# Window attention of the first layer: softmax scaling moved behind the value sums

## The reference

```python
xw = xp.reshape(Bx, nW, window, C)
qkv = (xw @ qkv_w + qkv_b).reshape(Bx, nW, window, 3, heads, hd)
q, k, v = (qkv[:, :, :, 0], qkv[:, :, :, 1], qkv[:, :, :, 2])
attn = jnp.einsum('bnqhd,bnkhd->bnhqk', q * scale, k)
attn = attn + bias[None, None]
...
attn = jax.nn.softmax(attn, axis=-1)
out = jnp.einsum('bnhqk,bnkhd->bnqhd', attn, v).reshape(Bx, nW, window, C)
out = out @ pw + pb
```

## Time and profile before

| | |
|---|---|
| median of 3 runs | 1364.43 us (1363.96 to 1365.02) |
| the profiled execution, timed from outside | 1360.38 us |
| its span, first to last instruction | 1358.6 us |
| mean granted TensorE clock | 0.839 of full |
| PE busy | 970.4 us, 71% |
| DVE busy | 899.0 us, 66% |
| ACT busy | 677.4 us, 50% |
| POOL busy | 593.5 us, 44% |
| transfers | 86481 packets, 142.11 MB |

### The profile page before, as it was taken

The page is one execution under the profiler, slowest core; times in us unless marked ns, Lnnn a source line. Parts: engine busy times, 40 slices in busy tenths (PEclk is TensorE's granted clock), DMA queues, the critical chain, the costliest instruction groups (busy, mean ns, idle before and its releaser), DMA issues.

```text
span 1358.6 us, 16130 instructions
## 1 busy us (share of the span) xinstructions
PE 970.4 (71%) x5318; PEld 521.5 (38%) x5318; DVE 899.0 (66%) x1366; ACT 677.4 (50%) x1009; POOL 593.5 (44%) x585
## 2 busy tenths in 40 slices
PE   5464466877777624377667778778999987677784
PEld 5221234544444312133222223226888852223231
DVE  6572766565666545968888865755666677876861
ACT  3221245454554332357667466664344346566674
POOL 6377545677784164453711456650000034706210
PEclk7776688788887865569788798978999998899999
DMA  7713445545565119224213352635655633544400
GB/s 244 260 43 110 136 102 154 154 131 157 145 161 144 64 34 115 35 41 67 43 23 48 53 95 45 113 85 124 212 192 193 205 74 67 88 62 63 72 21 13
DMA packets 86481, 142.11 MB, mean 105 GB/s; under 512 B 14973, under 2 KB 43774, under 8 KB 86398
## 3 DMA queue, kind: packets, MB, share of 16 engines
q1 hardware_dynamic: 77726, 123.50, 37.8%
q0 software_dynamic: 8192, 16.79, 5.0%
q10 hardware_dynamic: 480, 0.79, 0.5%
HBM read 58.17 MB, written 40.37 MB: 73 GB/s over the span
## 4 chain that ended last, share of the span: by engine, by line
PE 30%; DVE 11%; ACT 8%; DMA 5%; issue 4%; SPq 4%; POOL 3%; DVEq 0%; ACTq 0%; POOLq 0%
PE PS L915 7%; PE PS L874 5%; ACT P L982 5%; PE PS L934 5%; PE PS L892 4%; SPq L495 4%; DMA KS<-MAG 3%; PE PS L854 3%; DVE MX L1721 2%; PE PS L840 2%; DVE XNT L1462 2%; POOL A L1298 2%; PE PS L674 1%; PE PS L679 1%; ACT MAG L982 1%
## 5 line engine op out<-in xcount | busy, mean ns | idle before, releaser
L1721 DVE TENSOR_REDUCE MX<-PS 128x2 f32<-128x1024 f32 x256 | 306.5, 1222 | 123.4 <-PE PS L854 117.8
L982 ACT ACTIVATE P<-PS 128x1024 f32<-128x1024 f32 x256 | 262.4, 1025 | 168.4 <-PE PS L892 163.6
L854 PE MATMUL PS<-KS,QS 62*128 62x512 f32 x512 | 140.4, 546 | 69.7 <-DVE MX L1721 54.9
L1298 POOL DMA_INDIRECT A<-Y1D,POS x64 | 62.2, 972 | 273.4 <-DMA Y1D<-YE 186.7
L892 PE MATMUL PS<-QS,KS 64*128 64x512 f32 x512 | 125.9, 488 | 71.5 <-ACT P L982 68.9
L874 PE MATMUL PS<-P,V 128*32 128x512 f32 x1024 | 156.3, 686 | 0.1
L854 PEld LDWEIGHTS PS<-KS,QS 62*128 62x128 f32 x512 | 54.2, 209 | 211.3 <-DVE MX L1721 112.3
L915 PE MATMUL PS<-XRH,WH 128*128 128x512 f32 (+1 forms) x276 | 104.1, 419 | 0.0
L892 PEld LDWEIGHTS PS<-QS,KS 64*128 64x128 f32 x512 | 54.0, 206 | 122.7 <-ACT P L982 113.6
L773 PE MATMUL PS<-XST,WB 128*128 128x512 f32 x184 | 99.5, 683 | 0.0
L1317 POOL DMA_INDIRECT XS1D<-XN,POS x64 | 62.3, 973 | 63.2 <-DVE MX L1721 40.4
(11 more groups left out here) (220 smaller groups left out, 1854.8 us busy)
## 6 DMA issues: line engine op xcount, KB each, us to landing
WH<-W1SD SPq DMA_DIRECT2D x23, 704.0 KB, 4.8
WS<-WD SPq DMA_DIRECT2D x64, 200.0 KB, 4.2
QS<-EH SPq DMA_DIRECT2D x64, 128.0 KB, 4.3
KS<-EH SPq DMA_DIRECT2D x60, 128.0 KB, 5.8
WB<-in_wb SPq DMA_DIRECT2D x23, 322.0 KB, 2.9
XS<-XS0D SPq DMA_DIRECT2D x23, 256.0 KB, 4.2
Y0D<-YE SPq DMA_DIRECT2D x23, 256.0 KB, 4.3
XS<-XS1D SPq DMA_DIRECT2D x23, 256.0 KB, 3.8
```

The lines of the kernel that those rows point to most:

```text
L854: signal(pe.matmul(PS[:, s % 4, :], QS[rows, u % 3, hp, 128 * t:128 * t + 128], KS[rows, u % 3, hp, :], start=True, stop=True), "ms")
L982: act.activation(*a, **k).then_inc(sem[name], 1)
L1298: pool.indirect_dma_start(dst[:, k, t, :], None, src, bass.IndirectOffsetOnAxis(pos[:, k, g:g + 1], 0)).then_inc(sem[name], 16)
L1721: go("mx", dve.tensor_reduce(MX[:, u % 2, t].rearrange("p (o h) -> p o h", o=2)[:, :, hp], PS[:, s % 4 - 1:s % 4 + 1, :], AX.X, ALU.max))
```

## The change

The unscaled exponentials are spread. The sums and their reciprocals go to a new tile `REC` (two turns) instead of `WM`, and `even` is gone on both engines. A new function on SP, `spread_recips`, copies the reciprocals to the feature partitions in `RW`, again by seven and four transfers, now with rows of 20, 30 or 40 numbers. `window_out` multiplies the sums of the values by `RW` on VectorE, behind each of its two reductions. `spread` waits for the exponential where it waited for `even`. `window_max` of the next batch waits for the subtraction instead of `even`.

The table `MOVED` is changed as well. In the period of batch 4 the orders are now these. SP: store 14, passing 16, split 4, spread 4, spread_recips 4, store 15, passing 17, store 16, passing 18, store 17. GpSimd: large subtraction 4, products (4, 2), small subtraction 4, split 4, products (5, 0), norm step, products (5, 1), nine multiplications 4 (the two for the small windows each one place later). TensorE: head sum (5, 0) stands behind both halves of pass 17 instead of ahead of them; all else is as before. VectorE: the evacuation of head sum (5, 0) stands behind the clip of pass 17 instead of ahead of the tail's norm product. ScalarE: the weight split's copy stands one step earlier, ahead of the evacuation of sorted rows. Before batch 2, the split of weights 0 on GpSimd stands two scattering transfers earlier.

```diff
-LESS_AT, EXP_AT, SUM_AT, EVEN_AT, SPREAD_AT, OUT_AT = 11.5, 12, 13, 13.5, 14, 20
+LESS_AT, EXP_AT, SUM_AT, SPREAD_AT, RECIP_AT, OUT_AT = 11.5, 12, 13, 14, 15, 20
...
-            put(period * b + EVEN_AT, ("even", b, r))
...
+            REC = sb0("REC", [128, 2, 2, 40])
+            RW = sb0("RW", [128, 2, max(GRP)])
...
-        def even(eng, go, r, b):
-            eng.wait_ge(sem["wsum"], b + 1)
-            t = window_rows(r, b)
-            go("weven" + ("_v" if b < EARLY else ""),
-               eng.tensor_tensor(t, t, bc(WM[:, r], [128, 40, WIN[r]], 2), ALU.mult))
...
-                made(sp, "weven", b, 2)
+                sp.wait_ge(sem["wexp"], b + 1)
...
+            def spread_recips(b):
+                sp.wait_ge(sem["wsum"], b + 1)
+                for r in (1, 0):
+                    if b:
+                        sp.wait_ge(sem[f"wout{r}"], b)
+                    for s in range(4):
+                        rows = slice(32 * s, 32 * s + 32)
+                        if r:
+                            for p in range(2 if s < 3 else 1):
+                                at = WIN[1] * (4 * p + s)
+                                load(RW[:, 1, at:at + WIN[1]], bc(REC[rows, b % 2, 1, WIN[1] * p:WIN[1] * (p + 1)], [32, 4, WIN[1]], 1), "rec1")
+                        else:
+                            n, at = WIN[0] * (TURN0 + (s == 3)), WIN[0] * TURN0 * s
+                            load(RW[:, 0, at:at + n], bc(REC[rows, b % 2, 0, 0:n], [32, 4, n], 1), "rec0")
...
+                elif (what, *a[1:]) == ("window", RECIP_AT):
+                    spread_recips(a[0])
...
-                    made(dve, "weven", b - 1, 2)
+                    made(dve, "wsub", b - 1, 2)
...
-                    ins = dve.tensor_reduce(WM[:, r], window_rows(r, b), AX.X, ALU.add)
+                    ins = dve.tensor_reduce(REC[:, b % 2, r], window_rows(r, b), AX.X, ALU.add)
                 step(ins)
-                go("wsum", dve.reciprocal(WM[:], WM[:]))
+                go("wsum", dve.reciprocal(REC[:, b % 2], REC[:, b % 2]))
...
-                go(f"wout{r}", dve.tensor_reduce(WO[r][:], wide, AX.X, ALU.add))
+                step(dve.tensor_reduce(WO[r][:], wide, AX.X, ALU.add))
+                dve.wait_ge(sem[f"rec{r}"], 16 * (4, 7)[r] * (b + 1))
+                go(f"wout{r}", dve.tensor_tensor(WO[r][:], WO[r][:], RW[:, r, 0:GRP[r]], ALU.mult))
```

More of the change, by code:

```diff
@@ L64 @@
 BLOCKS_AT = SEND_AT + 72
-MOVED = {'POOL': {('window', 11): 0.1, 'send': -5.1, ('tail', 2): 1.0, ('qk', 6): -0.6, 'sub1': -1, ('qk', 5): -1, 'split': 3.5, 'mul0': 0.3, ('qk', 2): 1.3, ('less', 0): 1.1, 'mul1': -1.1, ('tail', 3): 0.1, ('even', 0): -0.9, ('less', 1): -1.3}, 'DVE': {('less', 0): 0.9, ('even', 0): 0.6, ('even', 1): 0.3, ('tail', 1): 0.7, 'yev': 1.4, ('window', 14): -1.5, ('qk', 9): 1.5, ('window', 18): 0.1, ('qk', 6): 0.4, ('window', 11): 1.0, ('qk', 8): 0.1, ('qk', 7): 0.3, ('window', 20): -0.6, 'clip': 0.1, 'act': 0.4, ('window', 13): 0.6, ('window', 10): -0.5, ('window', 7): -0.4, 'mul0': 1.5, ('qk', 0): 1.5, ('qk', 2): -0.3, ('less', 1): -1}, 'PE': {'down_e': 1.7, ('tail', 6): -1, ('window', 10): 1.5, ('tail', 7): -0.8, ('window', 8): 0.8, 'sorted': -3.0, ('tail', 1): -0.6, ('tail', 0): -0.7, ('tail', 4): 0.5, ('pair', 1): 1, ('window', 4): -0.4, ('window', 3): -0.1, ('window', 6): 0.1}, 'ACT': {('tail', 6): -1, ('tail', 2): 0.3, ('window', 3): 0.8, 'split': -2.3, 'sorted': -2.6, ('window', 12): 0.4, 'silu': 1, ('gate', 0): -0.4, ('tail', 5): -0.5, ('tail', 0): -0.6, ('tail', 4): -0.3}, 'plan': {'period': 9, 'step': 3, 'start': 1}, 'SP': {('window', 14): 2.1, ('pair', 0): 2.2, 'yev': 5.5, 'split': 5.4}}
@@ new lines @@
+MOVED = {'POOL': {('window', 11): 0.1, 'send': -5.1, ('tail', 2): 1.0, ('qk', 6): -0.6, 'sub1': -1, ('qk', 5): -1, 'split': 2.9, 'mul0': 0.6, ('qk', 2): 1.3, ('less', 0): -0.9, 'mul1': -1.1, ('tail', 3): 0.1, ('even', 0): 4.1, ('less', 1): -1.3, ('even', 1): 0.2}, 'DVE': {('less', 0): 0.9, ('even', 0): 2.6, ('even', 1): -1.5, ('tail', 1): 0.7, 'yev': 1.4, ('window', 14): -1.5, ('qk', 9): 1.5, ('window', 18): 0.1, ('qk', 6): 0.4, ('window', 11): 0.7, ('qk', 8): 0.1, ('qk', 7): 0.3, ('window', 20): -0.6, 'clip': 0.1, 'act': 0.4, ('window', 13): 0.6, ('window', 10): -0.5, ('window', 7): 1.7, 'mul0': 1.5, ('qk', 0): 1.5, ('qk', 2): -0.3, ('less', 1): -1, ('tail', 3): 0.6, 'mul1': -0.1}, 'PE': {'down_e': 1.7, ('tail', 6): -1, ('window', 10): 1.5, ('tail', 7): -0.8, ('window', 8): 0.9, 'sorted': -3.0, ('tail', 1): -0.6, ('tail', 0): -0.7, ('tail', 4): 0.5, ('pair', 1): 1, ('window', 4): -0.4, ('window', 3): -0.1, ('window', 6): 2.1}, 'ACT': {('tail', 6): -1, ('tail', 2): 0.3, ('window', 3): 0.8, 'split': -2.9, 'sorted': -2.6, ('window', 12): 0.4, 'silu': 1, ('gate', 0): -0.4, ('tail', 0): -0.6, ('tail', 4): -0.3, ('window', 4): 0.6, ('gate', 1): -0.1}, 'plan': {'period': 9, 'step': 3, 'start': 1}, 'SP': {('pair', 0): 0.2, 'yev': 2.0, 'split': 4.8, ('window', 15): -0.6}}
@@ L258 @@
     "GpSimd":
-        "prod rstd xi rstd0 x1_b split_lo pstep wsub weven wpv0 wpv1 rstd1 rat emb_k emb_q lo init_p",
+        "prod rstd xi rstd0 x1_b split_lo pstep wsub wpv0 wpv1 rstd1 rat emb_k emb_q lo init_p",
     "VectorE":
-        "init_v stats xn xi_raw prod_v wsub_v weven_v wpv0_v wpv1_v S_sb wmax0 wmax1 wsum wout0 wout1 "
+        "init_v stats xn xi_raw prod_v wsub_v wpv0_v wpv1_v S_sb wmax0 wmax1 wsum wout0 wout1 "
         "lsub hot eb pos gw gused lused gg lc a yev x1 h0 s_done gsum x0 step "
@@ L1264, in _ @@
                     less_max(pool, go, a[1], a[0])
-                elif what == "even" and a[0] >= EARLY:
-                    even(pool, go, a[1], a[0])
                 elif what in ("mul0", "mul1") and a[0] >= EARLY:
@@ L1613, in _ @@
                     less_max(dve, go, a[1], a[0])
-                elif what == "even" and a[0] < EARLY:
-                    even(dve, go, a[1], a[0])
                 elif what in ("mul0", "mul1") and a[0] < EARLY:
```

2 lines of the change are left out of this document (1 added, 1 removed).

## The result

The changed kernel takes 1382.3 us (median of four, 1375.5 to 1389.0) where the kernel before took 1364.2 us in the same comparison: a ratio of 1.0165, 95% interval 1.0124 to 1.0206, as the comparison gives it. The two medians alone divide to 1.0133, still inside the interval. The forecast was 1386. The profiled execution took 1385.4 us, its span is 1383.6 us against 1358.6.

The account below looks back on a forecast made before the run. Waits between engines, in two loops through GpSimd and SP's queue, were taken as the bound. Five periods (+19.1), the end (+5) and batch 1 (-2.3) gave +21.8 on the median of 1364.4: 1386.2 us, range 1377 to 1398.

Parts of the forecast that it names:

- The SP loop: Subtraction, spread, eleven new transfers (6.8 us), sorted rows for TensorE, next subtraction: 42.5 us instead of 36.65, taken for all periods.
- the backlog of the split: Weight-split transfers directly ahead of the spread on SP, over 1 MB in flight: up to 2.7 us more.
- the dear rival: SP's transfers cost 0.86 us each plus 2.7 us for the split: 1418 us; chance 0.13 for 1398 and more.
- The rule on dispatch: SP dispatches a transfer in about 50 ns, so the eleven cost about half a microsecond; kept as a rival.
- The long periods: Batch periods of 41.8 us with TensorE at low clock, set by GpSimd's chain alone: forecast to become 44.2 us.
- the GpSimd loop: Subtraction, GpSimd's products and multiplications, VectorE's sum, gates, scores, maximum: 36.65 to 39.5 us short, 41.8 to 44.2 long.
- The rival with a cheap queue: Eleven transfers cost SP next to nothing and GpSimd's chain decides: +11.5 us, 1376 us; chance 0.14.
- The head sum: TensorE's first score sum of the next batch, moved behind the gate matmuls, delays GpSimd's second product group by 2.6 us.
- The scalings at zero: Removing GpSimd's two scalings (2.50 us per batch) gains 0, because other waits hide them.
- The multiplications: VectorE multiplies by the reciprocals twice per batch, 0.3 us each; the first fits idle time, the second adds 0.3.
- Batch 1: Its spread can start about 165 instead of 176.76, so waits of VectorE and TensorE shrink: -2.3 us.
- The end: Behind the last batch the sorted rows' load is 6.6 us late, less 1.4 for two staging loads: +5 us.

Follow-up runs that it names:

- Experiment 1: Kernel before plus eleven more SP transfers directly behind each spread, copying constants into a tile nobody reads: 1381.0 against 1358.6 us, ratio 1.0171.
- 2: Changed kernel with the eleven reciprocal transfers moved on SP behind the next store and loads: 1367.5 us, ratio 1.0055.
- 8: Changed kernel with first score sum and SP's order as before, reciprocals spread by four transfers instead of eleven: 1456.4 us, ratio 1.0046 (second chip).
- experiment 10: Kernel before with only TensorE's first score sum moved behind the gate matmuls, its evacuation behind the clip, on the third chip: ratio 1.0042.
- Experiment 6: Kernel before without the two scalings of each batch, the spread waiting for the reciprocals instead: 1439.1 us, ratio 0.9934 (second chip).
- experiment 7: Changed kernel with late reciprocal transfers, first score sum back, and VectorE's multiplications by the reciprocals removed, waits kept: 1449.3 us, ratio 0.9996 (second chip).
- 5: Kernel before with only TensorE's first score sum moved behind the gate matmuls, its evacuation behind the clip: 1438.1 against 1447.0 us, ratio 0.9932 (second chip).

## Why the prediction was right, and where it was not

The forecast of 1386.2 was 3.9 us above the measured 1382.3. Step by step:

- **The SP loop.** Right in mechanism, and each part within 0.8 us, with errors to both sides. In the period of batch 4 the spread starts 6.2 us behind the subtraction (6.8 by the working), it takes 10.14 us against 9.46 before, the eleven 7.33 (6.8), the load is issued at 26.1 (about 26), TensorE has the rows at 30.15 (30.7), the rest is 11.70 (11.8), the period 41.85 (42.5). In the five periods the rows come 29.7, 31.7, 30.2, 30.3 and 30.9 us behind the subtraction, and the rest takes 11.0, 11.8, 11.7, 14.2 and 12.1. The row of a transfer of little data between SBUF tiles, 0.57 us, was the right neighbour; 0.67 was measured. (It copies four rows of 2 KB, and not eight short ones as the prediction has it.) Experiment 1 shows that this term alone carries the loss, and 2 that it is the place in the queue. One sign to look for was mis-sized: TensorE's idle time for the load is 5.80 us in this batch and not about 10, because its own work ahead of the rows also ended later, 24.35 us behind the subtraction and not 20.55. For the backlog of the split, up to 2.7 us in the dear rival, no row stood in the prediction; the spread took 0.7 us longer.
- **The rule on dispatch.** The Trainium skill ("DMA: Bandwidth & Descriptors", the table of the fixed cost) gives about 50 ns for the dispatch and calls descriptor generation small. The table stands in that page's section on a transfer that GpSimd issues, so the prediction stretched it when it took it for SP's. The changed kernel and experiments 1 and 8 measured 0.67 to 0.69 us of SP's time for each of these transfers, over ten times as much. By that rule experiment 1 would have been hardly slower than the kernel before.
- **The long periods.** 44.55 us in the period of batch 5, forecast as 44.2 on the GpSimd loop and then left out of the sum, which took 42.5 for all. There TensorE waited 2.27 us for VectorE behind the sorted rows, which fits the GpSimd loop being last. The five range from 40.7 to 44.6, 42.7 on average. The rival with a cheap queue was summed by another rule, three periods of the short kind and two of 44.2. By that rule the forecast's five periods are 215.9 us and its total near 1389.6, and the rival's pitch of 0.48 us comes to about 1383, not 1379. That 42.5 for all came closer, with 213.6 measured, is partly luck: one period was of the long kind and not two, and another took only 40.7.
- **The head sum.** The wait came out at 2.35 us where 2.6 was forecast. Its worth on the GpSimd loop was overrated: with the SP loop not late, that loop was to grow from 36.65 to about 39.2, and experiment 10 shows 37.9 to 38.2 for three periods, 39.6 for one, and 41.8 for the only long one, as before. In the short ones the norm step waits 0.67 us as before, so it takes up nothing. GpSimd's second group starts 14.7 us behind the subtraction instead of 12.5, 2.3 later, but its three products then take 2.50 us instead of 3.40 and the nine multiplications end only 1.3 us later, which is what the period grew. Why the products had taken longer was not tested. In the sum this did no harm because the SP loop was last; the rival with a cheap queue, 1376, was too high (experiment 10, which has the move and no further transfers, is at 1.0042, about 1370; experiment 2, with the change whole and the transfers at a cheap place, at 1.0055, about 1372).
- **The scalings at zero.** Right for the changed kernel, and for the reason given: GpSimd idles where they stood, and its norm step waits 2.91 us for ScalarE. The profile names no releaser for the first wait; ScalarE's last evacuation of the projected values ends at 305.22. In the changed kernel's trace:

```profile
305.36 3.32 POOL L457 TENSOR_TENSOR G<-QKV 128x400 f32<-128x400 f32 x4 [5.07 <-issue]
```

  Not right as a general statement. Experiment 6 gains 0.66% without them, since the spread may then start earlier and SP's loop no longer closes with the other. The eleven transfers take that slack and more.
- **The multiplications.** Mis-sized. 0.3 us was forecast for the second, on the path; it takes 1.26:

```profile
329.90 0.79 DVE L1498 TENSOR_TENSOR WO<-WO,RW 128x130 f32<-128x130 f32 x1
330.61 3.06 DVE L1496 TENSOR_REDUCE WO<-WS 128x140 f32<-128x2800 f32 x1
333.70 1.26 DVE L1498 TENSOR_TENSOR WO<-WO,RW 128x140 f32<-128x140 f32 x1
```

  The reason is in the last section. In a period that the GpSimd loop decides this would be about 1 us more than forecast; what it is worth alone was not measured, since experiment 7 did not isolate it.
- **Batch 1.** -2.3 us was forecast, 0 came. The spread did start ten microseconds earlier (166.78), and TensorE had its rows at 190.41 and not at 193.19. But there VectorE multiplies itself and is busy nearly without a gap until its XN operation, at 207.54 where it was 207.56 before. The wait of 2.38 us went, and in its place came three others: 1.07 us more for one clip, 0.59 for the two new multiplications, 0.74 more of waiting for ScalarE; 2.40 together. TensorE's idle time moved on to wait for VectorE:

```profile
208.28 1.90 PE L749 MATMUL PS<-WO,PROJ 128*32 128x130 f32 x16 [10.35 <-DVE XN L1538]
```

  The step that failed was to let the smaller of two waits decide, without asking which engine was next in line. How near to zero this term is one pair of traces can't say: the subtraction of batch 2 starts at 213.10 and 211.82 in the two traces of the kernel before, and between 209.6 and 215.1 in all ten traces outside the second chip.
- **The end.** +4.8 us where +5 was forecast.

So the sum of +21.8 stood against +25.0 in the spans: +20.2 in the periods (19.1), 0 in batch 1 (-2.3), +4.8 at the end (+5). The medians differ by 18.1 us. The profiled execution of the changed kernel was 3.1 us above its median and that of the kernel before 3.8 below, so the forecast was 3.9 us too high for the median (1386.2 against 1382.3) and 3.2 too low for the profiled execution (1382.2 against 1385.4).

## What to carry over

Price a queue of transfers by their number, with the duration of the nearest single one in the trace, and look for what stands behind them in the same queue: here eleven small transfers cost 1.7% ahead of one load that TensorE waits for, and of the changed kernel's loss two thirds went when they were put behind it. When a producer is moved on one engine, its consumer's place in another queue has to move with it, as the two orders of SP show. And where two loops are last by turns, a delay on either can cost something even if the other loop is longer on average: price each kind of period by the loop that is last in it.

## What was not expected of the hardware

**Some of VectorE's instructions are held until GpSimd's running one ends.** The same multiplication took 0.29 and 0.30 us in the period of batch 1, when GpSimd was idle, and 0.79 to 0.80 and 1.26 to 1.27 in those of batches 2 to 6. In the last period, with GpSimd idle again, the second took 0.30. The first, then GpSimd's timeline beside the multiplication of 333.70:

```profile
203.40 0.29 DVE L1498 TENSOR_TENSOR WO<-WO,RW 128x130 f32<-128x130 f32 x1
```

```profile
330.62 1.54 POOL L464 TENSOR_TENSOR WD<-WD,WM 128x800 f32<-128x800 f32 x1
332.24 2.57 POOL L457 TENSOR_TENSOR G<-QKV 128x700 f32<-128x700 f32 x2
```

VectorE's multiplication of 333.70 ends at 334.96, just behind GpSimd's products, which end at 334.81. The second of those two products starts at about 333.5, ahead of the multiplication. VectorE's sum of 330.61 reads one tile, ran across two of GpSimd's instructions and took its usual 3.06 us. A clip on VectorE, which reads one tile and two constants, was held too: 1.50 us in place of 0.42, until 319.61, with GpSimd's addition at 317.87 ending at 319.32:

```profile
317.77 0.42 DVE L1555 TENSOR_SCALAR UL<-UL 128x512 f32<-128x512 f32 x1
318.11 1.50 DVE L1558 TENSOR_SCALAR UL<-UL 128x512 f32<-128x512 f32 x1
```

The Trainium skill ("SBUF — State Buffer", section "SBUF: two separate sides") says that the two engines share a pair of ports that the instruction that starts first holds until its end. On VectorE's side this concerns its two-port modes and, against a GpSimd instruction that reads SBUF, operations with two inputs in SBUF. These rows agree: the multiplication ended 0.15 us and the clip 0.29 us behind GpSimd's instruction, and the sum was not held. A moved or added operation on VectorE must be priced by what GpSimd does at that moment: here 0.3 us alone, up to 1.27 beside it.

**Chips differ.** The kernel before takes 1358.6, 1447.0 and 1359.5 us on three chips, 6.5% apart, and one edit (5 and 10) came out 0.7% faster on one and 0.4% slower on another. In the four traces of the slow chip the mean granted TensorE clock is 0.80 to 0.82, in the ten others 0.82 to 0.85; nothing here tells whether that is the cause. A verdict of less than one per cent holds for the chip on which it was measured.
